# Tile 0's projections in one piece at the start of a local stage, and a feed-forward with two product buffers, splits on POOL and a reordered drain

## The reference

```python
x0 = layernorm(x)
a  = block_attention(x0)            # 16 heads of 8, blocks of 32 tokens, rotary, causal, softmax
y  = x0
for L in range(2):
    h = shift_token(y)              # upper 64 features come from the token before
    q, k, v = split(h @ wqkv[L])    # 8 heads of 64
    q, k = rotary_xpos(l2norm(q) * qs, l2norm(k) * ks)
    o = local_attention(q, k, v)    # windows of 64, each looks at itself and the one before
    y = y + o @ wo[L]
    h = layernorm(shift_token(y)) * g + b
    u, g = split(h @ w1[L] + b1[L]) # 2 x 341 columns
    y = y + (u * gelu(g)) @ w2[L] + b2[L]
out = x + a * silu(y)               # in the kernel: x_in + A_OUT * Silu(X)
```

## Time and profile before

| what | us |
|---|---|
| median of 3 runs | 882.16 (880.42 to 882.94) |
| the profiled execution: its own time | 883.38 |
| the profiled execution: its span | 881.6 |
| PE busy | 787.1 (89%) |
| DVE busy | 682.5 (77%) |
| ACT busy | 669.7 (76%) |
| POOL busy | 531.5 (60%) |

### The profile page before, as it was taken

How to read it: one execution, slowest core, us unless ns; L and a number is a source line. 1 busy time by engine, 2 the same in 40 slices (tenths; PEclk the granted TensorE clock), 3 DMA queues, 4 the chain that set the end, 5 groups by cost and what they waited for, 6 DMA issues and landing times. The chain is left out here.

```text
span 881.6 us, 26513 instructions
## 1 busy us (share of the span) xinstructions
PE 787.1 (89%) x9720; PEld 595.3 (68%) x9720; DVE 682.5 (77%) x1338; ACT 669.7 (76%) x2041; POOL 531.5 (60%) x505
## 2 busy tenths in 40 slices
PE   4788999878999999999779887999999999878985
PEld 1457777656888888887645545788888888654542
DVE  1577899789999999996234669999999999524455
ACT  2326777549999999998577526999999999747873
POOL 0364334169999999999200007999999999710000
PEclk8899999969999999999899988999999999989996
DMA  9120001002222222222101112222222222212001
GB/s 317 43 49 3 3 4 42 3 19 52 65 65 64 65 64 66 65 65 65 45 19 25 27 34 61 53 65 64 66 65 65 64 65 65 65 31 95 1 36 60
DMA packets 64707, 48.26 MB, mean 55 GB/s; under 512 B 40410, under 2 KB 50948, under 8 KB 64068
## 3 DMA queue, kind: packets, MB, share of 16 engines
q1 hardware_dynamic: 64580, 46.57, 20.9%
HBM read 10.63 MB, written 2.10 MB: 14 GB/s over the span
## 5 line engine op out<-in xcount | busy, mean ns | idle before, releaser
L422 PE MATMUL ps<-wqkv,split 128*128 128x512 f32 x576 | 188.5, 438 | 20.3 <-DVE tA L1157 13.4
L899 ACT ACTIVATE prob<-ps,nmax 128x128 f32<-128x128 f32 x512 | 179.3, 375 | 2.7 <-DVE nmax L1196 2.7
L1382 POOL TENSOR_TENSOR qr<-qr,ss 128x512 f32<-128x512 f32 x64 | 92.0, 1437 | 118.3 <-ACT ss L892 118.3
L1375 POOL TENSOR_TENSOR prob<-prob,rinv 128x512 f32<-128x512 f32 x128 | 133.2, 1042 | 29.1 <-DVE rinv L1203 28.9
L422 PEld LDWEIGHTS ps<-wqkv,split 128*128 128x128 f32 x576 | 98.7, 198 | 35.1 <-issue 25.0
L899 ACT ACTIVATION_READ_ACCUMULATOR prob<-ps,nmax 128x1 f32 x512 | 110.5, 216 | 0.0
L432 PE MATMUL ps<-ident,prob 128*128 128x128 f32 x640 | 97.2, 275 | 9.5 <-POOL prob L1375 9.2
L422 PE MATMUL ps<-split,w 128*128 128x512 f32 (+1 forms) x288 | 87.7, 447 | 15.9 <-DVE prob L1262 14.2
L1196 DVE TENSOR_REDUCE nmax<-ps 128x4 f32<-128x512 f32 x128 | 81.6, 677 | 11.8 <-PE ps L422 11.5
L432 PEld LDWEIGHTS ps<-ident,prob 128*128 128x128 f32 x640 | 76.0, 141 | 21.2 <-POOL prob L1375 13.0
L867 ACT ACTIVATE pT<-ps 128x512 f32<-128x512 f32 x128 | 80.7, 631 | 11.3 <-PE ps L432 11.1
(11 more groups left out here) (128 smaller groups left out, 1871.8 us busy)
## 6 DMA issues: line engine op xcount, KB each, us to landing
VB<-V SPq DMA_DIRECT2D x129, 128.0 KB, 2.3
kT<-kT SPq DMA_DIRECT2D x65, 128.0 KB, 2.3
XS<-X SPq DMA_DIRECT2D x32, 128.0 KB, 2.3
XS<-X SPq DMA_DIRECT2D x128, 32.0 KB, 1.9
D<-in_xT SPq DMA_DIRECT2D x8, 256.0 KB, 4.6
XS<-in_xT SPq DMA_DIRECT2D x2, 1024.0 KB, 6.1
out_T<-XS SPq DMA_DIRECT2D x8, 256.0 KB, 2.0
raw<-in_wqkv SPq DMA_DIRECT2D x2, 768.0 KB, 4.6
```

The lines of the kernel that those rows point to most:

```text
L422: return nc.tensor.matmul(o, l, r, start=start, stop=stop, skip_group_check=True)
L899: nc.scalar.activation(prob[:, m % 2, grp, s * P:(s + 1) * P], ps[:, 4 + grp, s * P:(s + 1) * P], ACT.Exp, bias=nmax[:, m % 2, col], accum ...
L1375: g.tensor_tensor(p4, p4, rinv[:, m % 2, 4 * grp:4 * grp + 4].unsqueeze(2).broadcast_to([P, 4, P]), ALU.mult).then_inc(l_prob[grp], 1)
L1382: g.tensor_tensor(hd(qr[:, m % 2, :]), hd(qr[:, m % 2, :]), ss[:, (base + m) % 2, 0:8].unsqueeze(2).broadcast_to([P, HEADS, HD]), ALU.mult ...
```

## The change

**Start of a local stage.** DVE splits tiles 0 to 3 in one piece (`first_split`; in L = 0 ahead of the last attention tiles but two). PE does q's, k's and v's projection of tile 0 one after the other, then the last attention tiles or the last down of the layer before, then q and k of tile 1. ACT's and DVE's pieces of tile 0 and 1 are ordered accordingly. SP's wait for the cleared columns moves from before the first window copies to the first copy of X.

**Feed-forward.** `hid` gets two buffers: parts 0 and 1 in `prob[:, j % 2]`, part 2 in the free memory `vexp`. `scaled(j)` writes tA and tB in turn, and both halves of the split go to POOL (`norm_high`, `norm_low`). ffn(j) on PE is now mean(j+2), up(j,0), variance(j+2), down(j-1), up(j,1), up(j,2); on ACT squares(j+2), Gelu(j,0), the other table, inverse_deviation(j+2), Gelu(j,1), Gelu(j,2); on DVE norm_centre(j+2), hidden(j,0), summed(j-1), scaled(j+2), hidden(j,1), hidden(j,2). w1's two parts are made at tiles 20 and 21 of the local stage. The seam has one mean before `local(30)`, up(0,0) before `local(33)`, and DVE's inverse sums of tiles 29 to 31 as early as ACT has them. The tables and the weights of the next layer's local stage are made one call later than before (ahead of ffn(5), ffn(6)).

**Drain.** Silu of chunks 0 to 4 in one piece on ACT behind Gelu(6,2), their products and sums on POOL; chunks 5 and 6 on DVE at the end; the last chunk's down, sum, Silu, gate and DMA in two halves of 256 columns (banks 7 and 0).

`tail` on DVE is now only `summed(CHUNKS - 1)`, on PE only `down(CHUNKS - 1)`, both at the start of the next local stage. `up(j, c)` holds the same six matmuls and waits as before. The diff, cut to its core:

```diff
+        hidx = vexp[:, :, 0:CHUNK]
+        GATE_POOL = 5
+        def hid(j, c):
+            return prob[:, j % 2, c, :] if c < 2 else hidx[:, j % 2, :]
@@ SP
+                        if L == 0 and m == 0:
+                            sp.wait_ge(zeros_made, 2)
...
-                    sp.wait_ge(zeros_made, 2)
                     sp.wait_ge(windows_zero, 1)
+                    sp.wait_ge(a_score, TILES)
...
-            for j in range(CHUNKS):
+            for j in range(CHUNKS - 1):
+                if j < GATE_POOL:
+                    sp.wait_ge(gate_first, made)
+                else:
+                    sp.wait_ge(gate_out, j - GATE_POOL + 1)
                 sp.dma_start(out[:, bass.ds(col, CHUNK)], x_in[:, bass.ds(col, CHUNK)]).then_inc(stored, 16)
...
@@ PE
                 if L == 0:
                     pe.wait_ge(a_sub, TILES)
-                    local(-3, 1)
+                q_projected(0)
+                k_projected(0)
+                v_projected(0)
+                if L == 0:
                     a_tile(TILES - 1, 1)
                     a_tile(TILES, 0)
-                    steps(-2, -2, local)
                 else:
-                    steps(-3, -2, local)
                     tail(CHUNKS, 0)
-                local(-1, 1)
-                steps(0, TILES - 2, local)
+                q_projected(1)
+                k_projected(1)
+                q_turned(0)
+                q_projected(2)
+                steps(0, TILES - 3, local)
...
...
+                def down(j, cols=slice(0, CHUNK), bank=7):
+                    wait(pe, x_new, x_before_ffn(L) + j)
+                    if bank == 0:
+                        pe.wait_ge(ln_log, nb + CHUNKS)
+                    for c, (u, n) in enumerate(PARTS):
+                        pe.wait_ge(ffn_hid, NPART * (fb + j) + c + 1)
+                        last = mm(ps[:, bank, cols], w2[0:n, c, :], hid(j, c)[0:n, cols], c == 0, c == NPART - 1)
+                    last.then_inc(ffn_y, 1)
+                def ffn(j):
+                    if j + 2 < CHUNKS:
+                        mean(j + 2)
+                    pe.wait_ge(ffn_lo, fb + j + 1)
+                    up(j, 0)
+                    if j + 2 < CHUNKS:
+                        variance(j + 2)
+                    down(j - 1)
+                    up(j, 1)
+                    up(j, 2)
+                mean(0)
+                local(TILES - 2, 0)
+                variance(0)
+                local(TILES - 1, 1)
+                mean(1)
+                local(TILES, 0)
+                variance(1)
+                bias_products()
...
+                pe.wait_ge(ffn_lo, fb + 1)
+                up(0, 0)
+                local(TILES + 1, 1)
+                mean(2)
+                local(TILES + 2, 0)
+                pe.wait_ge(x_new, x_before_ffn(L))
+                pe.wait_ge(bias_made, 1 + L)
+                up(0, 1)
+                variance(2)
+                up(0, 2)
+                for j in range(1, CHUNKS):
+                    ffn(j)
+                if L + 1 == DEPTH:
+                    for h in range(2):
+                        down(CHUNKS - 1, slice(h * CHUNK // 2, (h + 1) * CHUNK // 2), (7, 0)[h])
@@ ACT
+                q_squared(0)
+                k_squared(0)
+                if L == 0:
+                    a_tile(TILES - 1, 1)
+                norm_floor(0)
+                norm_log(0)
+                norm_inverse(0)
+                if L == 0:
+                    a_tile(TILES, 0)
+                q_squared(1)
+                local(-1, 1)
+                steps(0, TILES - 3, local)
...
+                def ffn(j):
+                    if j + 2 < CHUNKS:
+                        squares(j + 2)
+                    gelu(j, 0)
+                    if j + 2 < CHUNKS:
+                        load_exp_and_ln()
+                        inverse_deviation(j + 2)
+                    gelu(j, 1)
+                    gelu(j, 2)
+                squares(0)
+                local(TILES - 2, 0)
+                probs_copied(TILES - 3, 1)
+                inverse_deviation(0)
+                exponentials(TILES - 1, 0)
+                exponentials(TILES - 1, 1)
+                probs_copied(TILES - 2, 0)
+                o_copied(TILES - 3)
+                probs_copied(TILES - 2, 1)
+                squares(1)
+                probs_copied(TILES - 1, 0)
+                o_copied(TILES - 2)
+                inverse_deviation(1)
+                gelu(0, 0)
+                probs_copied(TILES - 1, 1)
+                o_copied(TILES - 1)
+                squares(2)
+                load_exp_and_ln()
+                inverse_deviation(2)
+                gelu(0, 1)
+                gelu(0, 2)
+                for j in range(1, CHUNKS):
+                    ffn(j)
+                    if L + 1 == DEPTH and j == CHUNKS - 2:
+                        for k in range(GATE_POOL):
+                            act.wait_ge(x_new, x_before_ffn(L) + k + 1)
+                            silu(k, slice(0, CHUNK))
...
@@ DVE
-            steps(23, TILES - 2, a_tile)
+            steps(23, TILES - 4, a_tile)
...
+                    first_split()
+                    steps(TILES - 3, TILES - 2, a_tile)
...
+                q_sin(0)
+                q_cos(0)
+                q_summed(0)
+                k_summed(0)
+                q_rotated(0)
+                if L == 0:
+                    a_tile(TILES - 1, 1)
+                k_scaled(0)
+                if L > 0:
+                    tail(CHUNKS + 1, 1)
+                q_sin(1)
+                q_cos(1)
+                local(-1, 1)
+                steps(0, 19, local)
+                ffn_weights_hi(L)
+                local(20, 0)
+                ffn_weights_lo(L)
+                steps(21, TILES - 3, local)
...
+                def ffn(j):
+                    if j + 2 < CHUNKS:
+                        norm_centre(j + 2)
+                    hidden(j, 0)
+                    summed(j - 1)
+                    if j + 2 < CHUNKS:
+                        scaled(j + 2)
+                    hidden(j, 1)
+                    hidden(j, 2)
+                norm_centre(0)
+                local(TILES - 2, 0)
+                inverse_sums(TILES - 3, 1)
+                inverse_sums(TILES - 2, 0)
+                inverse_sums(TILES - 2, 1)
+                v_copied(TILES - 1)
+                maxima(TILES - 1, 0)
+                maxima(TILES - 1, 1)
+                scaled(0)
+                added_to_x(TILES - 4)
+                inverse_sums(TILES - 1, 0)
+                norm_centre(1)
+                inverse_sums(TILES - 1, 1)
+                added_to_x(TILES - 3)
+                ffn_bias(L)
+                scaled(1)
+                hidden(0, 0)
+                added_to_x(TILES - 2)
+                norm_centre(2)
+                added_to_x(TILES - 1)
+                scaled(2)
+                hidden(0, 1)
+                hidden(0, 2)
+                for j in range(1, CHUNKS):
+                    if not gate and j == CHUNKS - 3:
+                        attn_tables(L + 1, 0)
+                        attn_tables(L + 1, 1)
+                    if not gate and j == CHUNKS - 2:
+                        attn_hi(L + 1)
+                        attn_lo(L + 1)
+                    ffn(j)
+                if gate:
+                    for k in range(GATE_POOL, CHUNKS - 2):
+                        gated(k, slice(0, CHUNK), k)
+                    gated(CHUNKS - 2, slice(0, CHUNK), CHUNKS - 2)
+                    for h in range(2):
+                        cols = slice(h * CHUNK // 2, (h + 1) * CHUNK // 2)
+                        summed(CHUNKS - 1, cols, (7, 0)[h], h)
+                        gated(CHUNKS - 1, cols, CHUNKS - 1 + h)
@@ POOL
+                def norm_high(j):
+                    pool.wait_ge(ln_scaled, fb + j + 1)
+                    wait(pool, ffn_a, (NPART * (fb + j - 1)) if j > 1 else 0)
+                    g.tensor_copy(split[:, j % 2, 0, :], (tA, tB)[j % 2][:]).then_inc(ffn_hi, 1)
+                def norm_low(j):
+                    pool.wait_ge(ffn_hi, fb + j + 1)
+                    g.tensor_tensor(split[:, j % 2, 1, :], (tA, tB)[j % 2][:], split[:, j % 2, 0, :].bitcast(F32),
+                                    ALU.subtract).then_inc(ffn_lo, 1)
+                for j in range(CHUNKS):
+                    norm_high(j)
+                    norm_low(j)
+                if L + 1 == DEPTH:
+                    for j in range(GATE_POOL):
+                        s, x = part(A_OUT, j, CHUNK), part(x_in, j, CHUNK)
+                        pool.wait_ge(gate_silu, j + 1)
+                        g.tensor_tensor(s, s, part(X, j, CHUNK), ALU.mult).then_inc(gate_pool, 1)
+                        pool.wait_ge(gate_pool, j + 1)
+                        g.tensor_tensor(x, x, s, ALU.add).then_inc(gate_first, 1)
```

More of the change, by code:

```diff
@@ L146, in build @@
         gel = (kA, kB, kn)
-        hid = prob[:].rearrange("p a b t -> p (a b) t")
         rstd = qr
```

(21 more changed lines are left out.)

240 lines of the change are left out of this document (87 added, 153 removed).

## The result

| | before | after | forecast |
|---|---|---|---|
| median, us | 882.55 (880.42 to 883.22, 4 runs) | 852.47 (851.53 to 853.97, 4 runs) | 849.5, range 836 to 865 |
| profiled execution, its span | 881.6 | 852.0 | |
| granted clock, mean | 0.954 | 0.976 | |

What follows compares the result with a forecast made beforehand. POOL and DVE fill the local stages' middle and PE nearly fills each chunk, so gains lie at seams. 5.3 - 0.5 + 9.1 + 5.4 - 0.5 + 13.9 = 32.7 off 883.4 gives 850.7, at the median 849.5; range 836 to 865.

Steps and rivals of the forecast that it cites:

- Seams: Local stage's end into feed-forward: scores(31) to first variance 28.4 us, PE idle some 2.5; each layer leads by 8.3 us.
- The clock term of 1.0 a layer: Behind PE's idle 2.5 us ahead of a feed-forward's first variance: 1.0 us a layer added for a slower clock.
- Rival B: Local-to-feed-forward transition: clock stays at 1.2 GHz through the first chunk, 6 us a layer, 1.5 per local start; 865, chance 0.23.
- Chunk: Middle of the feed-forward: 9.20 us from variance to variance against 9.12 before, longer than PE's own 8.66; eight such cycles.
- V + 4.4: Feed-forward cycle: Gelu(j,1)'s table load starts 4.4 us after variance(j+2) starts on PE, behind the gate half of up(j,1).
- wrong if a chunk is under 8.8: Sign against the forecast: a feed-forward chunk over 10 us or under 8.8, where 9.2 from variance to variance was expected.
- rival A: All seams go better: ring closes at PE's 8.66 (4.3), no clock loss (2.0), no POOL-DVE drain conflict (4.0); 839, chance 0.18.
- No price for hid's buffer and POOL's splits in the middle: Feed-forward middle: second hid buffer and splits moved to POOL buy nothing, 9.20 us a chunk against 9.12.
- Starts: Beginning of each local stage, from earlier projections and splits: 5.3 us gained in layer 0, 5.4 in layer 1.
- End of the local stage: Inverse sums made earlier let scores(31) start 2.3 us earlier; w1's parts at tiles 20 and 21 cost 0.5 a layer.
- Tables: Layer 0's feed-forward: next layer's tables on DVE between hidden(4,2) and norm_centre(7) add 2.5 us to the ring.
- Drain: Layer 1's end: last sum 29.2 + 4.0 us after the last variance, 4.0 for DVE gates beside POOL; 13.9 gained.

Runs made afterwards that it cites:

- the experiment with the sums of tile 1: Changed kernel with DVE making tile 1's sums, rotation, q(2) products and k_scaled(1) ahead of tile 4's split at both local starts: 853.55 us, ratio 0.9671.
- both edits: Inverse sums ahead of the first centre and w1's parts behind v_copied(30) and v_copied(31), added to the kernel with seam, tables and drain edits: 838.79 us, ratio 0.951.
- the experiment with three chunks: Changed kernel with POOL gating three drain chunks instead of five, DVE gating chunks 3 and 4 before hidden(7,0): 849.98 us, ratio 0.9629.
- the early split: Layer 1's first four tiles split after hidden(7,0), timed together with earlier mean(j+3) and centre, on top of the 838.79 us kernel: 833.9 us, ratio 0.9447.

## Why the forecast was right, and where it was not

- **Seams: right.** 28.3 us from scores(31) to the first variance for 28.4 forecast, with PE's gap of 2.50 where the walk had 2.5. The clock term of 1.0 a layer was 0 in the profile, 1.5 to 1.7 where it struck (six of 18 seams): some 0.6 on average. Rival B (clock at its lower level through the seam, 6 a layer) did not come: the granted clock is 1.00 from 751 to 763 us and from 782 to 786. No run puts the old seam or the old drain back; what they gain is read from the two profiles.
- **Chunk: the step that failed.** "Gelu(j,1) can start its table load at V + 4.4", behind PE's gate half, is wrong by the wait's place alone. The load starts at V + 3.2 and is hidden, and the cycle is 8.79: from the first to the last variance the two layers took 37.8 and 35.2 for 39.3 and 36.8 forecast, 3.1 more gained, and with the clock (2.0) and the drain (1.0) it is why the feed-forwards stand at +2.6 and +3.7 over the record. Swapping two lines made the forecast's 9.2 appear. So "wrong if a chunk is under 8.8" did come true by a hair, and with it the part of rival A that closes the ring near PE's work.
- **No price for hid's buffer and POOL's splits in the middle: right**, by one experiment each (not both at once). The ring that bounds the chunk is 8.79 and not the 9.20 of the record, but as forecast it holds neither of the two.
- **Starts: direction right, size off.** 5.3 and 5.4 on record; 4.4 and 3.0 by the profile, 4.4 and 2.9 by going back to the old start. q_scaled(0) came as forecast; what follows seems paced by DVE's whole load, as the experiment with the sums of tile 1 suggests.
- **End of the local stage: a cost not seen.** scores(31) did not come 2.3 earlier against normalised(0,1); that gain went into w1 (1.1, forecast 0.5) and into a centre that DVE makes ahead of local(30) and that waits for PE's mean while rinv(28,1) stands behind it (1.4). With both edits the stretch is 215.4, and the 2.3 against the 217.7 of before is there. The record asked what is queued behind a waiting instruction for PE's and POOL's queues, not for this one.
- **Tables: right** (2.5; measured 2.44).
- **Drain: right.** 32.4 to the last sum for 33.2. DVE's four operations took 6.34, 3.6 over 4 x 0.69 (forecast 4.0); that they wait by turns with POOL is borne out by the experiment with three chunks. The Trainium skill, "SBUF — State Buffer", "SBUF: two separate sides", has the two engines' shared ports held for a whole instruction by whichever of them starts first; the 0.69 and 1.77 of DVE's operation in that experiment agree. The 0.67 beside POOL's 1.93 agrees if the hidden before it, which still ran when POOL's record begins, kept the ports for DVE; the trace does not show who holds them.
- **Table load: right in size.** The Trainium skill, "ScalarE: Activation LUTs", "What ACT_TABLE_LOAD costs", would have had some 2.66 a switch; the activation follows 1.29 after the load's start here, too (802.94, 804.23).

In sum 31.6 gained behind the marker for 32.7 forecast; the span gained only 29.6, since the block attention lay 2.0 later in the changed kernel's profile. The sum was good by luck, because too little for the chunk (3.1), the clock (2.0) and the drain (1.0) stood against too much for starts (3.3) and local stages (4.0).

## What to carry to other kernels

Ask on which instruction each of several waits ends up when a table load goes ahead of an activation: write the wait that is met early last, so that the load carries it and runs beside the work it would wait for. A gap of 2.5 us of the matrix engine can cost more than its length, since the clock may fall behind it, so close it first and test other edits on top. In the start-up stretch here, with DVE busy for 94% of it, reordering DVE only moved the wait to the next tile; taking work out of the stretch, as the early split did, brought 1.2 to 1.6.

## What was not expected of the hardware

- Behind a gap of 2.50 in PE's work the granted clock either stayed at 1.0 or was 0.57 to 0.67 over the next 4 to 5 us, with the same instructions before the gap; behind 4.12 it was 0.50 over 4 us and 0.75 over the next 4. With the seam's gap cut to 0.32 none of eight seams lost time. No run here tells what decides between the first two.
- The rounded copy of 128x512 fp32 on POOL takes 0.61, half the 1.27 to 1.29 of a subtraction or product of two inputs of that size, and less than the 1.04 of POOL's products with a broadcast input.
- The first sixth of the program (the block attention up to the marker) varies by 3 us between profiles with nothing changed in it (marker at 143.3 to 146.4), more than several of the effects studied; comparing stretches from a common marker removes it.
